# First feed-forward of a two-layer decoder: both experts over all tokens, against tokens sorted by expert with register-addressed weights

## The chip, the cores and the metric

The kernel runs on one core of one Trainium2 chip, as one program with a queue of instructions for each engine: TensorE (PE in the profile), VectorE (DVE), ScalarE (ACT), GpSimd (POOL) and SyncE (SP), which here only issues DMAs. The queues meet only at semaphores. The metric is the device time of one execution in microseconds (us), as the median of several runs.

## The reference

The reference is a decoder of two layers on x of 16 x 64 tokens, 256 wide, in float32. Each layer is a token mixer, a cross-attention and a feed-forward, and each of the six stages is `x = x + stage(layernorm(x))`. The stage that matters here is the feed-forward of the first layer, a mixture of two experts with one picked for each token:

```
logits = x_flat @ w_router.T                       # 1024 tokens x 2
probs = softmax(logits); top_idx = argmax(probs); top_weight = probs[top_idx]
h = einsum('nd,ehd->enh', x_flat, w_fc)            # e = 2 experts, h = 1024, d = 256
a = square(where(h >= 0, h, 0.5 * h))
expert_out = einsum('enh,edh->end', a, w_proj)
mask = (top_idx == expert)
out = einsum('end,en->nd', expert_out, mask * top_weight)
```

It computes both experts for all tokens and keeps one. It is followed by the second layer's self-attention (16 heads of 16 channels, causal, in groups of 64 tokens), whose layernorm needs the feed-forward's result.

## The kernel before

Tokens stand as eight tiles `x[:, t, :]` of 128 rows. They form two halves of 512 (tiles 0 to 3 and 4 to 7) and four pairs g. A layernorm ln is done by pair: `ln_add` adds the stage's result to x and takes the statistics (DVE), `ln_rstd` takes the root (ACT), `ln_scale` writes `xn` (DVE), `ln_turn` transposes it (PE, four transposes for a pair), and `ln_turned` copies it to `xnT` (ACT). ln 2 stands ahead of the first feed-forward, ln 3 ahead of the self-attention.

The order on each queue is written out by hand. Every wait blocks all that stands behind it on the same queue.

Feed-forward before. It is in 32 steps n, sixteen for each half: eight blocks `hb` of 128 hidden units for expert 0, then eight for expert 1, on all 512 tokens of the half. `hidden(n)` (L1222) multiplies the 128 weights' columns by the tokens: 2 matmuls of 512 columns. `leaky(n)` on DVE takes two passes (L1752 and L1755), `hidden_squared(n)` on ACT the square (L682), and `expert_out(n)` (L1238) adds the block to the outputs of its expert in PSUM: 8 recorded instructions, that is 4 matmuls of 256 columns, for the four token tiles. The profile counts two instructions for each float32 matmul. After eight steps `add_expert` (L1762) adds the expert's result, times its weight, to x straight from PSUM. `w_e[e]` is the probability where the token picked expert e, and zero elsewhere. `route` computes the two logits on PE (L1206) and their difference on DVE (L1734 to L1739).

Around it. The cross-attention `cross(0, beside_x0)` runs nine turns `it`, and `beside_x0(it, place)` puts single steps of the norm, of `route` and of the first steps of the feed-forward between its work: `queries` L1074, `keys` L1079, `scores` L1121, `turn_probs` L1132, `context` L1146 and `project_out` L1158 on PE; `shift` L1688 to L1703 and `divide` L1711 to L1715 on DVE; `exps` L614 and `contexts` L655 on ACT. Behind the feed-forward comes the self-attention: `a_project` L1277, `a_values` L1287, then for i from 0 to 7 `a_scores` L1305, `a_shifts` L1831 to L1836 (DVE), `a_exps` L751 (ACT), `a_sums` L1842 (DVE), `a_turn` L1318, `a_turned` L758 (ACT) and `a_context` L1332. i = 0 to 3 belong to the first half, 4 to 7 to the second. POOL adds the bias `a_bo` to x in one instruction (L427) once ln 3 is complete. `weight_sum` (ACT, L771) needs the three weights of the last feed-forward.

All DMAs are issued by SP, most by the helper `load` (L297), in the order of its text. The first stage, a state-space scan, ends at about 280 us; the weight `wvT` of the cross-attention is loaded right behind it.

Of the kernel before, what the change touches and what calls it, by code (L numbers as in the profile page):

```python
# [15 lines left out]
U8 = mybir.dt.uint8  # L16
ALU = mybir.AluOpType
# [23 lines left out]
SHARED = (4, 9, 14)  # L41

# [22 lines left out]
def program(nc, io, out):  # L65
    ctx = ExitStack()
    with ctx:
# [27 lines left out]
        qkb = sb("qkb", [128, 4])  # L95
        ps = ctx.enter_context(nc.psum_tensor("ps", [128, 8, 512], F32))
        region = {"A": sb("region_a", [128, 48 * 256]), "B": sb("region_b", [128, 48 * 256]),
                  "C": sb("region_c", [128, 64 * 256]), "D": sb("region_d", [128, 4 * 256])}
        m_brows = nc.dram_tensor("m_brows", (NK * DST, TOK), F32).ap()
        m_rows = [nc.dram_tensor(f"m_rows{k}", (128, TOK), F32).ap() for k in range(NK)]  # L100
# [72 lines left out]
        f_fc = view("B", 0, [KH, 2 * HID])  # L173
        f_proj = view("B", 16, [2 * HB, D])
        f_neg = [view("C", 32 + 2 * i, [HALF]) for i in range(2)]
        f_leaky = [view("C", 36 + 2 * i, [HALF]) for i in range(2)]
        f_act = [view("C", 40 + 2 * i, [HALF]) for i in range(4)]
# [22 lines left out]
        def ln_bank(ln, g):  # L200

            return tiles2(2 + g % 2 if ln == 3 else g)
# [92 lines left out]
        def _(sp):  # L295
# [15 lines left out]
            load(small[:, 3:5], io["g"], "ld_const")  # L311
            load(qkb[:, :], io["a_bqk"], "ld_const")
            load(m_wout, io["m_wout"], "ld_wout")
# [15 lines left out]
            for u in range(NK * DST):  # L329
# [15 lines left out]
                if k == NK - 1 and n >= 2 and n < DST - 2:  # L345
# [4 lines left out]
                    if n < 6:  # L350
                        load(wk[:, piece], io["x0_wk"][:, piece], "ld_xqk")
                    else:
                        load(wq[:, n // 4 % 2, piece], io["x0_wq"][:, n // 4 % 2, piece], "ld_xqk")
            sp.wait_ge(sem("m_scan"), NK * DST - 1)
# [3 lines left out]
            for name, dst in (("f_router", f_router), ("f_fc", f_fc), ("f_proj", f_proj)):  # L358
                load(dst, io[name], "ld_f")
            sp.wait_ge(sem("ln_xn"), 3 * NT)  # L360
# [6 lines left out]
            for name, dst in (("x1_wvT", wvT1), ("x1_wo", wo1), ("x1_wqT", wqT1), ("x1_wkT", wkT1)):  # L367
                load(dst, io[name], "ld_x1")
            sp.wait_ge(sem("f_h"), 4 * HB)
            for i, name in enumerate(("t_gate", "t_up")):  # L370
                load(t_w[i], io[name], "ld_t")
            sp.wait_ge(sem("f_pr"), 4 * HB)
# [8 lines left out]
        def _(pool):  # L381
# [22 lines left out]
            for u in range(NK * DST - 1):  # L404
# [13 lines left out]
                if k < NK - 1:  # L418
# [4 lines left out]
                    if n == 12:  # L423
                        softplus_sum(k + 1)
            pool.wait_ge(sem("ld_a"), 80)
# [18 lines left out]
        def _(act):  # L444
# [233 lines left out]
            def hidden_squared(n):  # L678
                act.wait_ge(sem("f_leaky"), n + 1)
                if n >= 4:  # L680
                    act.wait_ge(sem("f_pr"), n - 3)
                act.activation(f_act[n % 4], f_leaky[n % 2], ACT.Square).then_inc(sem("f_act"), 1)  # L682
# [1400 lines left out]
```

## Time and profile before

| | |
|---|---|
| median of the runs (lowest, highest) | 960.12 us (959.73, 963.97) |
| the profiled execution's own time | 952.36 us |
| its span | 950.6 us |
| PE busy | 844.8 us (89%) |
| DVE, ACT, POOL busy | 574.7, 436.2, 280.7 us |
| first `hidden` to last `expert_out` | 521.2 to 650.2 us |

The profile is a page of tables and a trace that can be asked for more: a timeline of each engine with the idle time ahead of an instruction and what ended it, the chain of waits that ended last, busy time and granted TensorE clock by stretch, and the DMAs with their time to landing. All times count from the start of the span. Line numbers are those of the kernel before.

### The profile page before, as it was taken

To read this page: it belongs to the slowest core of one execution; us is meant where nothing else is said; L and a number is where in the kernel's file an instruction comes from. 1 tells how busy PE (TensorE), PEld (TensorE's weight loads), DVE (VectorE), ACT (ScalarE), POOL (GpSimd) and SP (SyncE) were. 2 spreads that over 40 slices of the span, in tenths; PEclk is the share of its full clock that TensorE was granted. 3 is DMA by queue.
4 is the path that set the end of the run, shared out by engine and by line. 5 is a ranking of instruction groups with operands and counts; after the bars stand their busy time and mean duration, and the time that the engine had idled before them with its cause. 6 is when DMAs were issued, how large, how long until landed. Compare 5 with 4: busy or idle time off the path is not lost.

```text
span 950.6 us, 12411 instructions
## 1 busy us (share of the span) xinstructions
PE 844.8 (89%) x5114; PEld 515.2 (54%) x5114; DVE 574.7 (60%) x703; ACT 436.2 (46%) x646; POOL 280.7 (30%) x128
## 2 busy tenths in 40 slices
PE   6687797876989899999999999999899899999977
PEld 3233243322445456665666666665788466656755
DVE  3799999899993332223533534545794443474686
ACT  3764655635515655555553221213555322232475
POOL 0189899898850000000000000001006992000000
PEclk9899999998999999999999999999879999999999
DMA  9566666667964000000000070003000000000001
GB/s 312 151 178 177 176 159 188 162 178 188 249 183 177 1 1 1 2 1 1 1 1 2 3 301 1 1 0 133 3 2 2 1 1 1 1 1 1 2 0 45
DMA packets 20120, 70.91 MB, mean 75 GB/s; under 512 B 3072, under 2 KB 4736, under 8 KB 18816
## 3 DMA queue, kind: packets, MB, share of 16 engines
q1 hardware_dynamic: 20064, 70.12, 25.2%
q8 instruction: 40, 0.66, 0.3%
q14 instruction: 16, 0.13, 0.0%
HBM read 66.31 MB, written 3.41 MB: 73 GB/s over the span
## 4 chain that ended last, share of the span: by engine, by line
PE 56%; DVE 15%; ACT 8%; DMA 8%; issue 6%; POOL 6%; SPq 0%; POOLq 0%; DVEq 0%; ACTq 0%
PE ps L1158 10%; PE ps L1074 9%; PE ps L1238 6%; PE ps L1222 6%; DMA region_b<-m_rows 5%; PE ps L1121 3%; POOL region_c L410 3%; PE ps L1146 3%; DMA region_c<-m_rows 3%; PE ps L1079 2%; DVE ps L1641 2%; DVE region_c L1646 2%; PE ps L963 2%; PE ps L1048 2%; PE ps L915 2%
## 5 line engine op out<-in xcount | busy, mean ns | idle before, releaser
L410 POOL TENSOR_TENSOR region_c<-region_c,region_b 128x1024 f32<-128x1024 f32 x42 | 102.8, 2455 | 57.1 <-DMA region_b<-m_rows 46.1
L427 POOL TENSOR_TENSOR x<-x,region_a 128x2048 f32<-128x2048 f32 x1 | 4.5, 4530 | 382.1 <-DVE xn L1555 382.1
L963 PE MATMUL ps<-region_c,ident 128*128 128x512 f32 x168 | 86.8, 644 | 16.8 <-POOL region_c L410 8.5
L1646 DVE TENSOR_TENSOR_SCAN region_c<-region_c,ps 128x1024 f32<-128x1024 f32 x43 | 97.8, 2282 | 2.4 <-ACT ps L559 1.2
L1158 PE MATMUL ps<-region_c 128*128 128x256 f32 x384 | 90.1, 381 | 0.0
L1158 PEld LDWEIGHTS ps<-region_c 128*128 128x128 f32 x384 | 72.4, 190 | 25.0 <-issue 16.8
L1723 DVE COPY region_b<-ps 128x512 f32<-128x512 f32 x32 | 21.5, 689 | 86.9 <-PE ps L1132 86.8
L1641 DVE TENSOR_TENSOR ps<-ps,region_c 128x1024 f32<-128x1024 f32 x52 | 63.2, 1215 | 5.6 <-PE ps L951 5.5
L963 PEld LDWEIGHTS ps<-region_c,ident 128*128 128x128 f32 x168 | 33.1, 204 | 55.3 <-issue 35.4
L1074 PE MATMUL ps<-xnT,region_a 128*128 128x512 f32 x128 | 61.5, 603 | 0.8 <-ACT region_c L627 0.8
L1238 PE MATMUL ps<-region_b,region_c 128*128 128x256 f32 x256 | 60.6, 379 | 0.0
L1222 PE MATMUL ps<-xnT,region_b 128*128 128x512 f32 x128 | 60.2, 593 | 0.0
L1238 PEld LDWEIGHTS ps<-region_b,region_c 128*128 128x128 f32 x256 | 48.6, 190 | 20.1 <-issue 14.9
L1074 PE MATMUL ps<-xnT,region_c 128*128 128x512 f32 x128 | 58.6, 594 | 0.7 <-ACT region_c L655 0.7
L682 ACT ACTIVATE region_c<-region_c 128x512 f32<-128x512 f32 x32 | 20.2, 630 | 84.2 <-DVE region_c L1755 84.2
L1752 DVE TENSOR_SCALAR region_c<-ps 128x512 f32<-128x512 f32 x32 | 22.1, 691 | 55.1 <-PE ps L1222 55.0
L410 POOL TENSOR_TENSOR region_b<-region_c 128x1024 f32<-128x1024 f32 x21 | 51.5, 2453 | 11.8 <-DVE region_c L1646 11.8
L553 ACT ACTIVATE region_c<-region_c,a_log 128x1008 f32<-128x1008 f32 x43 | 47.9, 1127 | 10.0 <-DVE region_c L1646 9.9
L963 PE MATMUL ps<-region_b,ident 128*128 128x512 f32 x84 | 43.6, 643 | 9.7 <-POOL region_b L410 5.4
L951 PE MATMUL ps<-region_b,sel_b 96*128 96x512 bf16 x104 | 32.4, 395 | 21.3 <-DVE region_c L1646 21.2
L1646 DVE TENSOR_TENSOR_SCAN region_c<-region_a,ps 128x1024 f32<-128x1024 f32 x21 | 47.9, 2282 | 2.7 <-issue 1.4
L619 ACT ACTIVATE region_c<-ps 128x512 f32<-128x512 f32 x32 | 19.1, 597 | 64.8 <-PE ps L1074 64.8
(222 smaller groups left out, 1608.5 us busy)
## 6 DMA issues: line engine op xcount, KB each, us to landing
region_b<-m_rows SPq DMA_DIRECT2D x43, 512.0 KB, 5.1
region_c<-m_rows SPq DMA_DIRECT2D x21, 512.0 KB, 5.4
xn<-m_brows SPq DMA_DIRECT2D x12, 512.0 KB, 4.5
region_a<-in_x_wo SPq DMA_DIRECT2D x2, 2048.0 KB, 13.1
m_rows<-region_b SPq DMA_DIRECT2D x4, 512.0 KB, 6.0
region_a<-in_x_wq SPq DMA_DIRECT2D x8, 256.0 KB, 6.8
region_b<-in_f_fc SPq DMA_DIRECT2D x1, 2048.0 KB, 7.9
region_b<-in_f_proj SPq DMA_DIRECT2D x1, 2048.0 KB, 12.9
```

The lines of the kernel that those rows point to most:

```text
L410: pool.tensor_tensor(m_hc[u % 3], m_h[u % 3], m_cb[u % 3], ALU.mult).then_inc(sem("m_hc"), 1)
L553: act.activation(m_da[u % 3][:, :, 1:S], m_delta[k % 2][:, :, 1:S], ACT.Exp, scale=a_log[:, k, n:n + 1]).then_inc(sem("m_da"), 1)
L951: last = pe.matmul(ps[:, 2 * (u % 2) + c, :], sel_b[:, u % 32, :], m_sb[:, u // 32, c * HALF:c * HALF + HALF], start=True, stop=True)
L963: last = pe.matmul(ps[:, 4 + c, :], ident[:, :], m_hc[u % 3][:, c * HALF:c * HALF + HALF], start=(n == 0), stop=(n == DST - 1))
L1074: last = pe.matmul(b, w, xnT[:, k, cols(it)], start=(k == 0), stop=(k == KH - 1))
L1121: last = pe.matmul(ps[64 * (b % 2):64 * (b % 2) + 64, 4 + a // 2, c:c + S], q_T[:, a, S * b:S * b + S], keys_T[:, S * b:S * b + S], start= ...
L1146: last = pe.matmul(banks[r].rearrange("p (s a q) -> p s a q", s=2, a=4)[:, s], ctxn[64 * r:64 * r + 64, 4 * (it // 4) + 2 * m + s, :], mov ...
L1158: last = pe.matmul(tiles2(2 * (it // 4) + t // 2)[:, t % 2, :], o_Ts[layer][it % 2][:, a, 128 * t:128 * t + 128], wvo[:, 4 * (it % 4) + a, ...
L1222: last = pe.matmul(ps[:, 4 + n % 4, :], f_fc[:, k, HID * e + 128 * hb:HID * e + 128 * hb + 128], xnT[:, k, c * HALF:c * HALF + HALF], star ...
L1238: last = pe.matmul(tiles2(2 * e + t // 2)[:, t % 2, :], f_act[n % 4][:, 128 * t:128 * t + 128], f_proj[:, HB * e + hb, :], start=(hb == 0 ...
L1641: dve.tensor_tensor(inputs(u), inputs(u), m_du, ALU.mult).then_inc(sem("m_dbu"), 1)
L1646: dve.tensor_tensor_scan(m_h[u % 3], m_da[u % 3].rearrange("p b t -> p (b t)"), inputs(u), 0.0, ALU.mult, ALU.add).then_inc(sem("m_scan"), 1)
```

## The change

Only the first feed-forward, and what is interleaved with it, is changed. Each half of 512 tokens is now sorted by picked expert. A half takes five tiles of 128 rows, each with tokens of one expert alone (rows that get no token are filled with ones), in whatever way the tokens split. The steps are ten jobs s, five for each half.

- `route(half)` is longer by three operations (the pick, a running count over the four tiles, and what was picked in earlier tiles). `count(half)` on PE counts by three small matmuls with a triangle of ones, and `places(half)` on DVE makes of it, in nine small operations, the row that each token takes (`f_row`) and for each tile the address of its expert's weights (`f_weights_at`).
- POOL scatters the rows of `xn` to DRAM (`scatter`, four indirect DMAs for each half, 128 rows of 1 KB each). SP loads the five tiles back (`sorted_rows`, 640 KB), PE transposes them (`sorted_turn`, ten transposes for each half), ACT copies them (`sorted_turned`).
- `hidden(s)` has the tokens stationary and the weights moving: 4 matmuls of 512 columns. The weights' columns are chosen by a register that PE reads with `value_load`. `leaky(s)` is two passes on DVE of 128x1024. `turn_leaky(s)` is eight transposes on PE, `squared(s)` two squares of 128x512 on ACT, `down_rows(s)` 8 matmuls of 256 columns on PE, `result(s)` a copy of 128x256 on ACT.
- SP stores each result to DRAM, POOL gathers the rows of a half back into `xn` (`gather`, four indirect DMAs), and `add_back(half)` on DVE adds them to x, times the probability. `add_expert` and its weights are gone.
- The DRAM rows are first filled with ones by two DMAs of 640 KB, which SP issues ahead of the load of `wvT`.
- Loads `x1_wo`, `t_gate` and `t_up` wait for the last `hidden`; the other x1 weights are issued behind the store of job 4.
- ln 3 for the first half is done in jobs 7 to 9, for the second half behind `a_scores(2)`, `a_context(0)` and `a_turn(1)`; `a_project(4)` to `a_project(7)` and `a_values(1)` move behind `a_context(1)`.

```diff
+            def count(half):
+                pe.wait_ge(sem("f_pick"), half + 1)
+                b = sort_bank(half)
+                pe.matmul(b[:, 16:20], f_before, small[:, 32 + 4 * half:36 + 4 * half], start=True, stop=False)
+                pe.matmul(b[:, 16:20], ones[:, :], small[:, 84:88], start=False, stop=True)
+                pe.matmul(b[:, 24:25], ones[:, :], small[:, 83:84], start=True, stop=True).then_inc(sem("f_count"), 1)
...
+            def expert_rows(s):
+
+                if s % SORTED == 0:
+                    pe.wait_ge(sem("f_row"), s // SORTED + 1)
+                weights_at.append(pe.value_load(f_weights_at[0:1, s:s + 1], min_val=0, max_val=WEIGHTS))
...
-                for k in range(KH):
-                    last = pe.matmul(ps[:, 4 + n % 4, :], f_fc[:, k, HID * e + 128 * hb:HID * e + 128 * hb + 128],
-                                     xnT[:, k, c * HALF:c * HALF + HALF], start=(k == 0), stop=(k == KH - 1))
+                    pe.wait_ge(sem("f_leaky"), s - 1)
+                expert_rows(s)
+                for c in range(2):
+                    for k in range(KH):
+                        last = pe.matmul(ps[:, 4 + 2 * (s % 2) + c, :], f_xT[h][:, j, k, :],
+                                         f_fc[:, bass.ds(weights_at[s] + (HID * k + HALF * c), HALF)],
+                                         start=(k == 0), stop=(k == KH - 1))
                 last.then_inc(sem("f_h"), 1)
...
-                for t in range(4):
-                    last = pe.matmul(tiles2(2 * e + t // 2)[:, t % 2, :], f_act[n % 4][:, 128 * t:128 * t + 128],
-                                     f_proj[:, HB * e + hb, :], start=(hb == 0 and t % 2 == 0),
-                                     stop=(hb == HB - 1), skip_group_check=True)
+                for hb in range(HB):
+                    last = pe.matmul(ps[:, 2, 0:D], f_aT[s % 2][:, hb, :],
+                                     f_proj[:, bass.ds(weights_at[s] + D * hb, D)],
+                                     start=(hb == 0), stop=(hb == HB - 1))
                 last.then_inc(sem("f_pr"), 1)
...
+            for s in range(2, JOBS - 1):
+                turn_leaky(s)
+                hidden(s + 1)
+                if s == 3:
+                    sorted_turn(1, 0)
+                if s == 4:
+                    sorted_turn(1, 2)
+                if s == JOBS - 2:
                     ln_turn(3, 0)
-                    ln_turn(3, 1)
-                hidden(n)
-                expert_out(n - 2)
...
+                down_rows(s)
+                if s == 3:
+                    sorted_turn(1, 1)
+            pe.wait_ge(sem("ln_T"), 4 * 3 + 1)
+            ln_turn(3, 1)
+            turn_leaky(JOBS - 1)
...
+            def scatter(h):
+                pool.wait_ge(sem("f_fill"), 32)
+                pool.wait_ge(sem("ln_xn"), 2 * NT + 4 * (h + 1))
+                pool.wait_ge(sem("f_row"), h + 1)
+                for t in range(4 * h, 4 * h + 4):
+                    pool.indirect_dma_start(f_in[h], bass.IndirectOffsetOnAxis(ap=f_row[:, t:t + 1], axis=0),
+                                            xn[:, t, :], None).then_inc(sem("f_sent"), 16)
...
             dve.wait_ge(sem("ld_a"), 80)
             a_values(0)
-            ln_scale(3, 2)
-            ln_scale(3, 3)
             a_shifts(0)
             a_shifts(1)
             a_sums(0)
+            add_back(1)
+            ln_add(3, 2)
+            ln_add(3, 3)
+            a_shifts(2)
+            a_sums(1)
+            ln_scale(3, 2)
+            ln_scale(3, 3)
+            a_shifts(3)
+            a_sums(2)
             a_values(1)
```

## Rows read from the trace of the kernel before

**Rows 1.** The page: the span, busy time by engine, granted clock in 40 slices.

```profile
span 950.6 us, 12411 instructions
PE 844.8 (89%) x5114; PEld 515.2 (54%) x5114; DVE 574.7 (60%) x703; ACT 436.2 (46%) x646; POOL 280.7 (30%) x128
PEclk9899999998999999999999999999879999999999
```

**Rows 2.** The chain that ended last, 480 to 760 us: start, us, what.

```profile
582.38 1.73 PE ps L1238 x8
584.11 1.72 PE ps L1222 x4
```

**Rows 3.** Timeline of PE: start, us, instructions, idle before and its releaser.

```profile
292.11 1.88 PE L1074 MATMUL ps<-xnT,region_a 128*128 128x512 f32 x4
493.49 1.84 PE L1206 MATMUL ps<-region_b,xnT 128*128 128x2 f32 x16
514.21 7.17 PE L1158 MATMUL ps<-region_c 128*128 128x256 f32 x32
614.93 1.04 PE L898 MATMUL ps<-ident,xn 128*128 128x128 f32 x8
615.81 1.88 PE L1222 MATMUL ps<-xnT,region_b 128*128 128x512 f32 x4
653.77 3.72 PE L1287 MATMUL ps<-region_b,xnT 128*64 128x256 f32 x32
```

**Rows 4.** The line L1214 (a wait inside `hidden`): when PE's queue passed it.

```profile
L1214 PEldq EVENT_SEMAPHORE  x2: 51/51/51, 517.4 to 523.3; - x2
```

**Rows 5.** Timeline of DVE, 509 to 712 us.

```profile
509.72 0.16 DVE L1735 TENSOR_TENSOR small<-small,ps 128x4 f32<-128x4 f32 x1
641.83 0.69 DVE L1752 TENSOR_SCALAR region_c<-ps 128x512 f32<-128x512 f32 x1 [2.03 <-PE ps L1222]
650.45 1.66 DVE L1762 SCALAR_TENSOR_TENSOR x<-ps,small,x 128x256 f32<-128x256 f32 x4 [7.20 <-PE ps L1238]
658.14 1.37 DVE L1555 TENSOR_SCALAR xn<-x,mv,rstd 128x256 f32<-128x256 f32 x4
659.43 1.22 DVE L1831 TENSOR_TENSOR region_c<-ps,region_a 128x1024 f32<-128x1024 f32 x1
661.93 3.33 DVE L1836 TENSOR_TENSOR region_c<-region_c 128x1024 f32<-128x1024 f32 x1
686.16 1.23 DVE L1831 TENSOR_TENSOR region_c<-ps,region_a 128x1024 f32<-128x1024 f32 x1 [1.17 <-PE ps L1305]
704.30 1.23 DVE L1831 TENSOR_TENSOR region_c<-ps,region_a 128x1024 f32<-128x1024 f32 x1 [0.89 <-PE ps L1305]
```

**Rows 6.** Timeline of ACT, 660 to 680 us.

```profile
671.38 1.06 ACT L751 ACTIVATE region_c<-region_c 128x1024 f32<-128x1024 f32 x1 [1.19 <-DVE region_c L1836]
673.75 1.09 ACT L758 ACTIVATE region_c<-ps 128x512 f32<-128x512 f32 x2 [1.31 <-PE ps L1318]
```

**Rows 7.** Timeline of POOL, 640 to 760 us.

```profile
659.66 4.53 POOL L427 TENSOR_TENSOR x<-x,region_a 128x2048 f32<-128x2048 f32 x1 [382.07 <-DVE xn L1555]
```

**Rows 8.** DMAs: issues with KB each and median us from issue to landing.

```profile
out_x<-x SPq DMA_DIRECT2D x8, 128.0 KB, 1.9
region_b<-in_a_wqkv SPq DMA_DIRECT2D x1, 768.0 KB, 4.3
region_a<-in_x_wvT SPq DMA_DIRECT2D x1, 1024.0 KB, 5.8
```

**Rows 9.** Timeline of SP: start and duration of the issue of `wvT`.

```profile
274.13 0.33 SPq L297 DMA_DIRECT2D region_a<-in_x_wvT  x1
```

**Rows 10.** Stretches of PE: us, busy (instructions), granted clock, DMA share, GB/s.

```profile
678.00:680.00 2.00, 0.60 (x36) 1.00 0.03 8
682.00:684.00 2.00, 2.00 (x32) 0.59 0.03 8
702.00:704.00 2.00, 2.00 (x68) 0.79 0.01 4
```

More of the change, by code:

```diff
@@ L200, in ln_bank @@
         def ln_bank(ln, g):
[L202 removed]
+            if ln == 2 and g >= 2:
+                return tiles2(3 if g == 2 else 1)
+            if ln == 3:
+                return tiles2(2 if g == 2 else 3)
+            return tiles2(g)
         t_w = [view("B", 8 * i, [2048]) for i in range(3)]
@@ L1251, in beside_x0 @@
                     ln_turn(2, 1)
-                if (it, at) == (7, "head 1"):
+                if (it, at) == (7, "begin"):
                     route(0)
+                if (it, at) == (7, "head 2"):
+                    count(0)
+                if (it, at) == (8, "head 2"):
+                    sorted_turn(0, 0)
+                    sorted_turn(0, 1)
                 if (it, at) == (8, "turn"):
@@ L1256, in beside_x0 @@
                 if (it, at) == (8, "context"):
-                    hidden(1)
+                    sorted_turn(0, 2)
                 if (it, at) == (9, "begin"):
-                    expert_out(0)
-                    hidden(2)
-            pe.wait_ge(sem("ld_const"), 64)
+                    turn_leaky(0)
+            pe.wait_ge(sem("ld_const"), 96)
             pe.wait_ge(sem("ld_xqk"), 192)
@@ L1393, in _ @@
                 a_context(i - 2)
+                if i == 3:
+                    pe.wait_ge(sem("ln_T"), 4 * 3 + 4)
+                    for n in range(4, 8):
+                        a_project(n)
+                    a_values(1)
+                    pe.wait_ge(sem("a_qk"), 8)
                 if i <= 8:
                     a_turn(i - 1)
+                if i == 2:
+                    pe.wait_ge(sem("f_y"), JOBS)
+                    ln_turn(3, 2)
+                    ln_turn(3, 3)
                 if i == 6:
@@ L1857, in a_divide @@
                     last.then_inc(sem("a_o"), 1)
-            ln_add(3, 2)
-            ln_add(3, 3)
+            ln_add(2, 2, sem("x0_out"))
+            ln_add(2, 3, sem("x0_out"))
+            ln_scale(2, 2)
+            ln_scale(2, 3)
+            leaky(1)
+            route(1)
+            places(1)
+            route_weights(0)
+            for s in range(2, JOBS):
+                leaky(s)
+                if s == 4:
+                    route_weights(1)
+                if s == 7:
+                    add_back(0)
+                    ln_add(3, 0)
+                    ln_add(3, 1)
+                if s == 8:
+                    ln_scale(3, 0)
+                    ln_scale(3, 1)
             dve.wait_ge(sem("ld_a"), 80)
             a_values(0)
-            ln_scale(3, 2)
-            ln_scale(3, 3)
             a_shifts(0)
```

379 lines of the change are left out of this document (234 added, 145 removed).

## The prediction

> **What bounds the kernel now.** I read the page first, then the chain of waits, then PE's timeline of the stage, and at last the other engines where PE leaves it. The page shows PE busy in 89% of the span, and no other engine over 60% [rows 1]. In the feed-forward the chain is PE alone: steps of 1.72 and 1.73 us alternate with no gap [rows 2], so a pair `hidden`, `expert_out` costs 3.45 us. DVE waits 2.03 us for PE ahead of each of its steps [rows 5]. 32 pairs are 110.4 us. Behind the stage the picture is another one: from `a_scores` on, DVE's passes of 1.22 us, ACT's `a_exps` of 1.06 us and PE take turns [rows 5, 6], and PE is at half its clock (1.2 GHz) from about 682.8 to 702.8 us, after a stretch in which it was busy for 0.60 of 2 us [rows 10]. So two questions decide: how many us of PE work go, and whether the self-attention can start as much earlier as PE does.
>
> **The PE work, part by part.** PE's time goes by the columns of the moving operand: 1024 columns cost 1.72 us, whether as 2 x 512 or as 4 x 256 [rows 2]. A job has 4 x 512 in `hidden` and 8 x 256 in `down_rows`: 3.44 + 3.46 = 6.90 us. Four transposes cost 615.81 - 614.93 = 0.88 us [rows 3], so `turn_leaky` costs 1.76 us. A job is 8.66 us, ten are 86.6 us. The sorted rows cost 20 transposes, 4.4 us. `count` is three matmuls of a few columns; the eight matmuls of `route` take 1.7 us [rows 3], so three take 0.6 us, twice 1.2 us. Sum 92.2 us against 110.4: PE has 18.2 us less to do. `route` only moves.
>
> **Do the other engines keep up within a job?** PE's order is `turn_leaky(s)`, `hidden(s+1)`, `down_rows(s)`. `leaky(s+1)` is two passes of 128x1024 at 1.22 us [rows 5]; with 0.3 us of semaphores some 2.8 us, behind `down_rows` of 3.46 us. Margin 0.6 us. ACT's squares are 2 x 0.55 us [rows 6], with `hidden` of 3.44 us as cover. DVE's extra work in job 7 is `add_back(0)`, 1.66 us (priced as `add_expert`, the same operation), and statistics of two pairs, about 2.2 us; 5.9 us are free between two `leaky`. All of this I put at zero. If `leaky` took 1 us more, 0.4 us a job would show, 4 us in all.
>
> **The way through DRAM at the start.** No row shows an indirect DMA. `places(0)` ends about 502.7 us on the clock of before: `count(0)` lies at 500 us, and nine operations of 0.16 to 0.2 us follow [rows 5]. Then four indirect DMAs, their landing (a store of the same 128 KB lands after 1.9 us), an issue, and a load of 640 KB (768 KB land after 4.3 us) [rows 8]. PE needs the rows behind `project_out(6)` of the third head, about 520.5 us (514.21 plus three quarters of 7 us, plus `count`) [rows 3]. So 17.8 - 1.9 - 0.4 - 4.3 = 11.2 us are left for four issues, 2.8 us each. Bounds from the rows: 0.33 us (a plain issue by SP) [rows 9] and 4.53 us (POOL's longest instruction) [rows 7]. I take 1.5 us, since 128 row addresses are more than SP's issue and far less than a pass over 128x2048: hidden. At 4.53 us each, 7 us would show. In the second half the load stands behind the store of job 2 on SP, which I place about 5 us before PE asks for it: issues and 4.3 us of landing leave 0 to 1.5 us of stall, taken as 0.8. The first steps are ordered anew around `project_out(7)`: `sorted_turn(0, 0)` and `(0, 1)` and two jobs' work fill PE, and waits there come to about 1 us more than before. The fill of 1.3 MB ahead of `wvT` costs nothing: it lands at 274.13 + 5.8 = 279.9 and PE starts the cross-attention at 292.11 [rows 3, 8, 9], so there are 12 us of room; by the 768 KB in 4.3 us the fill takes some 7 us.
>
> So `a_values(0)`, at 653.77 us before [rows 3], comes 18.2 - 0.8 - 1.3 = 16.1 us earlier, at 637.7.
>
> **Registers.** PE must read ten values from SBUF before the matmuls that use them, and compute addresses. What may hide it: PE's queue passed the wait of `hidden(0)` at 517.4 us [rows 4], while the matmuls of `hidden(0)` started at 521.2, so the queue runs 3.8 us ahead where no wait holds it. In a job it is held at `turn_leaky`, for `leaky`, which is free 0.6 us before the array is, and 1.76 us of transposes follow: some 2.4 us, less 0.8 to 1.0 us to issue them, cover about 1.4 us of the read. Bounds: 0.05 us (a wait in that queue) [rows 4], and above by 4.3 us, a whole DMA [rows 8]. I take it as hidden, being nearest to the queue's own rows. The Trainium skill (Runtime: NRT & Kernel Launch, "The ~15µs preamble/postamble breakdown") gives 1.3 us for a register load from HBM, which would be just under this cover; no row here shows one.
>
> **What the tail gives back.** From 637.7 us: `a_values(0)` to 641.4, `a_scores(0)` to 642.6. DVE runs `a_shifts(0)` and `a_shifts(1)` to 650.1 (3 passes of 1.25 us each), `a_sums(0)` to 651.3, `add_back(1)` to 653.0, statistics to 655.0, then, by the written order, `a_shifts(2)` and `a_sums(1)` to 659.9, and only now `ln_scale(3, 2)`, with 0.7 us for its first pair (1.37 us for four tiles [rows 5]). PE is done with `a_turn(1)` at 654.5 and stands at `ln_turn(3, 2)` until 660.6: an idle time of 6 us. The two turns, `a_scores(3)` and `a_context(1)` take it to 664.9, four `a_project` to 671.8, of which one waits about 1.8 us for ACT's copies, `a_values(1)` of 3.7 us and `a_turn(2)` to 678.4, `a_scores(4)` to 679.6. `a_shifts(4)` starts at 679.7; before, it starts at 686.16 [rows 5]. Of 16.1 us, 6.5 are left. What was hidden in PE's surplus before is now DVE's order: `add_expert` was 1.66 us too, but it stood ahead of the attention, with no `a_shifts(2)` between it and `xn`.
>
> The gather isn't late: result 9 is stored by 637.3 (634.7 + 0.4 for the copy, 0.3, 1.9), DVE asks for the rows at 651.3, so each of four indirect DMAs may take 3 us.
>
> Clock. PE stood nearly still about 678.6 to 682 us before, and the half clock followed [rows 10]. The new idle time of 6 us is longer, so I expect the same there, with `ln_turn(3, 2)` to `a_project(5)` at 1.2 GHz: up to 3 us, less the 1.8 us in which PE waits for ACT anyway, about 1.5 us. In return i = 4 to 7 may run at 2.4 GHz. Before, 686.16 to 704.30 us took 18.1 us [rows 5]; DVE alone needs 3 x 4 passes of 1.24 us plus a division of about 2 us, 16.9 us. So -1.2 us to 1.5 us, and I set the two against each other: net 0.
>
> Sum: -6.5 us on a profiled execution of 952.36 us, 945.9 us. The profiled one ran 0.8% under the median of 960.12 us; the same ratio gives 953.6 us.
>
> A rule that speaks against the change, weighed: POOL's bias add from 659.66 to 664.19 stretched a DVE pass that reads two SBUF operands from 1.24 to 3.33 us [rows 5, 7]. The Trainium skill (SBUF — State Buffer, "SBUF: two separate sides") says that the two engines exclude each other for whole instructions, and that descriptors of GpSimd's DMAs can't be written meanwhile. By it, each gather could wait for one pass of `a_shifts` and each scatter for a copy, 4 x 1.24 = 5 us, which the 12 us of room would still take; by the rows alone it is 0.
>
> **Rivals.**
> 1. Register work shows on PE. For it: the cover of 1.4 us is thin and repeated in all jobs. Against it: the queue's lead of 3.8 us. A read of 2.4 us shows 1 us in 9 jobs: +9 us, 962.6 us. From a read of 2.7 us on, the kernel is slower than before by over 0.5%; at 3.2 us 970.
> 2. The way through DRAM is late, the rival on the other side: at over 2.8 us for an indirect DMA PE stands at `sorted_turn(0, 0)`, at over 3 us DVE at `add_back(1)`. At 4.53 us: 7 + 6 = 13 us, 966.6 us, slower. It decides from about 4.2 us.
> 3. The tail gives nothing back, because DVE's passes overlap better than I walked them: up to -16 us, 944 us. Against it: the order on DVE's queue is fixed, so at most part of it.
> 4. The change doesn't make PE's work less as counted: matmuls with an address from a register run slower. 12 in a job, 0.1 us each: +12 us, 965.6 us. Nothing in the trace shows such a matmul.
>
> **How the numbers follow.** Forecast (small gain, 950 to 957 us) 0.55; rival 1 0.18; rival 2 0.10; rival 3 0.10; rival 4 0.07. The range of 948 to 967 us leaves out most of rival 3 and the far ends of 1 and 2. A measurement here tells 0.5% (4.8 us) from no change: faster is below 955.3 us, slower above 964.9 us. Faster: four fifths of the forecast and all of rival 3, 0.54. Slower: half of rivals 1 and 4, most of rival 2, 0.21. The rest, 0.25, is within 0.5%.
>
> **What would show it.** Right: jobs of 8.7 us on PE without gaps; `a_values(0)` near 638 us; an idle time of some 6 us ahead of `ln_turn(3, 2)` put down to DVE's `ln_scale`; the second half's first `a_shifts` near 680 us. Wrong: gaps ahead of each `hidden` with nothing released by another engine (rival 1), PE waiting for a DMA at the first sorted transposes or DVE at `add_back(1)` (rival 2), longer matmuls (rival 4), or an `a_shifts(4)` at 670 us (rival 3).

## The result and the profile after

| | before | after |
|---|---|---|
| median (lowest, highest) | 959.92 us (950.94, 963.97) | 944.95 us (938.76, 948.89) |
| profiled execution, its span | 952.36, 950.6 us | 948.89, 947.0 us |
| PE busy | 844.8 us | 827.5 us |
| `shift(7)` on DVE, the last of the cross-attention, start | 514.37 us | 517.99 us |
| `a_values(0)` on PE, start | 653.77 us | 635.99 us |
| `a_shifts(4)` on DVE, start | 686.16 us | 679.01 us |

The changed kernel takes 0.9863 of the time of before, with an interval of 0.9821 to 0.9904: 1.4% faster, some 13 us. The forecast was 953.6 us with a range of 948 to 967 us, so the direction was right and the gain was larger than the range allowed. Repeats on two chips gave 944.22 us, ratio 0.9879 [0.9851, 0.9907], and 942.09 us, ratio 0.9858 [0.9820, 0.9895]. The gain is 10 to 15 us by medians.

The page of the kernel after, its counterpart to [rows 1]: span, busy time, granted clock in 40 slices, the DMAs with KB and us to landing (POOL's have no KB).

```profile
span 947.0 us, 12500 instructions
PE 827.5 (87%) x5077; PEld 509.5 (54%) x5082; DVE 554.3 (59%) x669; ACT 434.3 (46%) x650; POOL 296.5 (31%) x144
PEclk9899899998999999999999999995889999999989
f_in<-ones SPq DMA_DIRECT2D x2, 640.0 KB, 6.5
region_a<-f_in SPq DMA_DIRECT2D x2, 640.0 KB, 5.2
f_in<-xn,f_row POOLq DMA_INDIRECT x8, 2.4
```

PE is busy for 17.3 us less. The clock's row has 5, 8, 8 where before has 9, 8, 7: PE ran longer at half clock in the self-attention.

PE's timeline of the feed-forward, after (start, us, line, count, idle before and its releaser). L1369 is `turn_leaky`, L1353 `hidden`, L1379 `down_rows`, L1328 `sorted_turn`:

```profile
531.27 1.13 PE L1242 MATMUL ps<-region_b,ctxn 64*128 64x256 f32 x8 [0.82 <-DVE region_b L1883]
533.64 1.13 PE L1242 MATMUL ps<-region_b,ctxn 64*128 64x256 f32 x8 [1.23 <-ACT region_c L721]
553.97 0.38 PE L1311 MATMUL ps<-small,sort 128*128 128x4 f32 x2 [0.51 <-DVE small L1900]
554.93 5.39 PE L1353 MATMUL ps<-region_b,region_a 128*128 x8
560.16 3.62 PE L1379 MATMUL ps<-region_b,region_c 128*128 x16
563.62 1.04 PE L1369 MATMUL ps<-ident,region_c 128*128 128x128 f32 x8
564.49 3.60 PE L1353 MATMUL ps<-region_b,region_a 128*128 x8
571.38 1.04 PE L1369 MATMUL ps<-ident,region_c 128*128 128x128 f32 x8
578.63 0.87 PE L1328 MATMUL ps<-ident,region_a 128*128 128x128 f32 x4 [2.78 <-DMA region_a<-f_in]
579.30 5.13 PE L1379 MATMUL ps<-region_b,region_c 128*128 x16
```

A job is 571.38 - 563.62 = 7.76 us, without a gap. Of it `turn_leaky` is 0.87 us, not the 1.76 us of the forecast. The two `hidden` and `down_rows` at 5.39 and 5.13 us ran partly at 1.2 GHz, each behind a short rest of PE. The wait of 2.78 us is for the load of the second half's sorted rows, which SP issued behind the store of job 2 (L393). The issue alone took 2.17 us:

```profile
571.99 0.32 SPq L393 DMA_DIRECT2D f_out<-region_c  x1
572.41 2.17 SPq L315 DMA_DIRECT2D region_a<-f_in  x1
```

This wait, and where the half clock falls, differ from execution to execution. The first repeat of the changed kernel has:

```profile
575.68 0.66 PE L1328 MATMUL ps<-ident,region_a 128*128 128x128 f32 x4 [1.15 <-DMA region_a<-f_in]
576.17 3.62 PE L1379 MATMUL ps<-region_b,region_c 128*128 x16
```

There the wait is 1.15 us and the `down_rows` behind it runs at full clock. So does `hidden(2)` (3.70 us), behind the same rest of 0.52 us; the half clock fell some 20 us earlier, behind the rests of 0.82 and 1.23 us. The second repeat has a wait of 1.95 us and a `down_rows` of 5.31 us.

The tail, where the self-attention begins (PE, then DVE, after):

```profile
635.99 3.72 PE L1432 MATMUL ps<-region_b,xnT 128*64 128x256 f32 x32
642.19 1.21 PE L1450 MATMUL ps<-region_c 32*64 32x64 f32 x64 [1.33 <-DVE region_c L1983]
645.88 1.94 PE L1463 MATMUL ps<-ident,region_c 128*128 128x128 f32 x8 [2.49 <-ACT region_c L818]
658.54 1.94 PE L994 MATMUL ps<-ident,xn 128*128 128x128 f32 x8 [4.32 <-DVE xn L1715]
664.21 8.93 PE L1422 MATMUL ps<-xnT,region_b 128*128 128x512 f32 x16
657.66 1.37 DVE L1715 TENSOR_SCALAR xn<-x,mv,rstd 128x256 f32<-128x256 f32 x4
679.01 1.23 DVE L1983 TENSOR_TENSOR region_c<-ps,region_a 128x1024 f32<-128x1024 f32 x1 [1.49 <-PE ps L1450]
```

PE stands idle for 4.32 us at `ln_turn(3, 2)` (L994) until DVE's `ln_scale` (L1715), at the place and by the releaser that the forecast named. From `a_values(0)` to `a_shifts(4)` it is 43.0 us; before it was 32.4 us [rows 3, 5], and the forecast had 42.0 us. The two repeats have 44.9 and 43.7 us for it.

The clock there (stretches of PE after: us, busy, granted clock, DMA share, GB/s), to set beside [rows 10]:

```profile
640.00:644.00 4.00, 2.06 (x121) 0.97 1.00 407
644.00:648.00 4.00, 2.12 (x16) 0.50 1.03 421
664.00:668.00 4.00, 4.00 (x17) 0.54 0.02 4
688.00:692.00 4.00, 4.00 (x124) 0.50 0.02 4
```

PE was busy for half of 640 to 644 us. It then ran at 1.2 GHz for 24 us, and again from about 685 to 694 us.

**Where the profiled pair differs.** Split at `shift(7)`, which lies ahead of all the changed PE work but for the first `count`: entry 3.6 us later after; from there to `a_shifts(4)` 171.8 us before and 161.0 us after, so 10.8 us shorter; from `a_shifts(4)` to `a_shifts(7)` 18.1 and 17.8 us; from `a_shifts(7)` to the end 246.3 and 250.2 us. Sum: 3.6 - 10.8 - 0.3 + 3.9 = -3.6 us, the difference of the spans. Of the 3.6 us, 0.6 us are the first `count`. The rest, and the 3.9 us, lie in code that didn't change, and come with short dips of the granted clock that some executions have and others don't. So this pair probably understates the gain. That isn't certain for the 3.9 us: from `a_shifts(7)` to the end both profiled kernels with the old feed-forward take 246.3 us, and the twelve with the new one (without extra scatters) 246.4 to 250.7 us, most of them over 248 us. The stage itself is compared from `shift(7)` on below.

### The profile page after: what moved, and what is told of

Read it like the earlier page. It is cut to its first block, busy times and chain, and to the rows that moved or that the text cites. A ratio compares the mean times of both kernels' runs of the same rounds, so it can differ in the third digit from the quotient of the medians.

```text
span 947.0 us, 12500 instructions
## 1 busy us (share of the span) xinstructions
PE 827.5 (87%) x5077; PEld 509.5 (54%) x5082; DVE 554.3 (59%) x669; ACT 434.3 (46%) x650; POOL 296.5 (31%) x144
## 4 chain that ended last, share of the span: by engine, by line
PE 55%; DVE 16%; DMA 9%; ACT 8%; issue 6%; POOL 6%; SPq 0%; POOLq 0%; DVEq 0%; ACTq 0%
PE ps L1254 11%; PE ps L1170 9%; DMA region_b<-m_rows 5%; PE ps L1217 4%; PE ps L1379 4%; PE ps L1353 3%; PE ps L1242 3%; DMA region_c<-m_rows 3%; POOL region_c L454 3%; PE ps L1175 2%; DVE region_c L1806 2%; DVE ps L1801 2%; POOL region_b L454 2%; PE ps L1059 2%; PE ps L1422 2%
## 5 line engine op out<-in xcount | busy, mean ns | idle before, releaser
L475 POOL DMA_INDIRECT f_in<-xn,f_row x8 | 8.0, 994 | 276.3 <-DVE f_row L1917 274.5
L685 ACT ACTIVATE region_c<-ps 128x512 f32<-128x512 f32 x32 | 19.1, 597 | 66.6 <-PE ps L1170 66.6
L1011 PE MATMUL ps<-xnT,region_b 128*128 128x512 f32 (+1 forms) x96 | 45.9, 611 | 0.7 <-ACT xnT L526 0.7
L688 ACT ACTIVATE region_c<-ps 128x512 f32<-128x512 f32 x32 | 19.1, 597 | 58.4 <-PE ps L1170 58.4
L1848 DVE TENSOR_TENSOR region_c<-ps,small 128x1024 f32<-128x1024 f32 x8 | 9.8, 1225 | 54.4 <-PE ps L1217 54.4
L721 ACT ACTIVATE region_c<-ps 128x512 f32<-128x512 f32 x48 | 25.4, 598 | 34.8 <-PE ps L1242 34.8
L501 POOL TENSOR_SCALAR region_b<-region_b,small 128x512 f32<-128x512 f32 x12 | 25.1, 2088 | 49.2 <-PE ps L1488 49.2
## 6 DMA issues: line engine op xcount, KB each, us to landing
region_a<-in_x_wo SPq DMA_DIRECT2D x2, 2048.0 KB, 10.8
```

Source lines behind the costliest of these rows:

```text
L1011: last = pe.matmul(ps[0:rows, pair_at + c, :], lhs(k), (rhs if rhs is not None else xnT[:, k, :])[:, c * HALF:c * HALF + HALF], start=(k = ...
```

## The experiments

In what follows "from `shift(7)`" is the time from the start of that pass (`divide` and the feed-forward follow it) to the start of the `a_shifts` named, in the profiled execution. It is 145.1 us to `a_shifts(0)` and 171.8 us to `a_shifts(4)` before; 122.9 and 161.0 us after. In the first repeat of the changed kernel it is 120.1 and 159.0 us, and that repeat is what the variants are compared with. The second repeat has 122.6 and 160.5 us, so a difference of 2 us between two profiles can be chance. "The tail" is the stretch from `a_values(0)` to `a_shifts(4)`: 32.4 us before, 43.0, 44.9 and 43.7 us in the three profiles of the changed kernel.

> The changed kernel again, as the base for the others on the same chip. Theory T: the job is 7.76 us, since eight transposes cost 0.88 us and not 1.76, and a half clock falls where PE stands idle. Expected: 12 to 14 us below the kernel before. Rival R (the gain of the first runs was luck of the clock): 6 to 8 us below.

Measured: 944.22 us, ratio 0.9879 [0.9851, 0.9907], 10.3 us below by medians. That is less than theory T expected and more than the rival did.

**1. The transposes, doubled.**

```diff
-                    for a in range(4):
+                    for a in (0, 1, 2, 3) * 2:
```

> Each of the eight transposes of turn_leaky is written twice; the output is unchanged. T (0.11 us a transpose, PE is the limit through all jobs): a job of 8.64 us, a_values(0) about 8.8 us later, the time 7 to 9 us above the changed kernel. Rival (0.22 us a transpose, as the prediction had it): 17 us more. Rival (the tail is set by DVE and swallows it): under 3 us more.

Measured: 946.74 us, ratio 0.9921 [0.9896, 0.9947], 2.5 us more by medians. PE's timeline:

```profile
559.42 1.91 PE L1369 MATMUL ps<-ident,region_c 128*128 128x128 f32 x16
568.05 1.91 PE L1369 MATMUL ps<-ident,region_c 128*128 128x128 f32 x16
573.90 0.66 PE L1328 MATMUL ps<-ident,region_a 128*128 128x128 f32 x4 [0.50 <-DMA region_a<-f_in]
```

Sixteen transposes take 561.16 - 559.42 = 1.74 us, 0.109 us each, and a job 568.05 - 559.42 = 8.63 us. That is the job of the forecast (8.66 us), with twice the transposes that the kernel has. So the size of the error is shown. The time moved less than the 8.7 us of work: 5.5 us to `a_shifts(0)`, 5.2 us to `a_shifts(4)`, 2.5 us by medians. Part of it went into rests that were there anyway: the wait for the sorted rows is 0.50 us where the repeat has 1.15 us, and the rest of 0.52 us ahead of `count(1)` is gone. Another part is chance: the repeat ran two short rows ahead of `project_out(7)` at half clock, 1.6 us longer, and this run didn't. The expected 7 to 9 us of time were wrong.

**2. The load of the second half's rows, one store earlier.**

```diff
-            for s in range(3):
+            for s in range(2):
...
-            for s in range(3, SORTED):
+            for s in range(2, SORTED):
```

> SP issues the load of the second half's sorted rows ahead of the store of job 2 instead of behind it. T: PE's wait of 2.8 us at sorted_turn(1, 0) is gone, and with it the half clock of the 5 us behind it, 3 to 4.5 us lower. Rival (the load is late for the scatter's sake): the wait stays, within 1 us.

Measured: 942.86 us, ratio 0.9872 [0.9849, 0.9895]. The wait is gone:

```profile
573.46 0.60 PE L1328 MATMUL ps<-ident,region_a 128*128 128x128 f32 x4
573.89 3.62 PE L1379 MATMUL ps<-region_b,region_c 128*128 x16
```

From `shift(7)` it is 118.7 us to `a_shifts(0)` and 156.7 us to `a_shifts(4)`, 1.4 and 2.3 us less than in the repeat. By medians it is 1.4 us less, which the intervals don't separate from nothing. The expected 3 to 4.5 us counted on the wait and the slow `down_rows` of the first profile, and the repeat has only the 1.15 us of wait.

**3. Addresses written out in place of the register.** The three first jobs of a half take expert 0 and the last two expert 1, whatever the tokens picked.

```diff
-                weights_at.append(pe.value_load(f_weights_at[0:1, s:s + 1], min_val=0, max_val=WEIGHTS))
+                weights_at.append(WEIGHTS * (s % SORTED >= 3))
```

> The changed kernel with constants in place of the register: value_load is left out, the first three tiles of each half take expert 0's weights and the last two expert 1's, so the result is right for tokens whose tile happens to have that expert only; all other work is the same. T (PE's queue runs ahead, a register operation is 46 ns): jobs of 7.76 us as before, the time within 1 us of the changed kernel. Rival 1 of the prediction (register work shows): jobs shorter by 0.5 us or more, 5 us lower.

Measured: 941.06 us, ratio 0.9860 [0.9824, 0.9895]; the kernel with registers has 0.9879 and 0.9858. A job takes 7.76 us here too (`turn_leaky` starts at 562.76 and 570.52 us), so inside the jobs the registers cost nothing. From `shift(7)` it is 119.2 us to `a_shifts(0)` against 120.1 us. The rows of the kernel after for the lines of the read and of `hidden`: duration in ns (min, median, max), first and last start.

```profile
L1338 PEldq TENSOR_LOAD <-f_weights_at x10: 298/302/490, 524.6 to 615.4; - x10
L1353 PEldq FUSED_REGOPS  x40: 42/46/51, 525.5 to 616.4; - x40
L1353 PE MATMUL ps<-region_b,region_a x80: 592/592/1145, 525.8 to 619.8; 128*128 x80
```

A read is 0.30 us and an address 0.046 us, both in PE's queue, under a cover that the forecast put at 1.4 us. The matmul itself takes 0.592 us (median), and with a fixed address 0.592 us too.

**4. The old kernel with less PE work and its own tail.** One of eight blocks of hidden units is left out for each expert, so 4 of 32 pairs, 13.8 us by the 3.45 us of a pair.

```diff
+FB = HB - 1
...
-                c, e, hb = n // (2 * HB), n // HB % 2, n % HB
+                c, e, hb = n // (2 * FB), n // FB % 2, n % FB
```

> The kernel before with seven of the eight hidden blocks of each expert (one eighth of the first feed-forward's hidden units is left out): 28 steps for 32, 13.8 us less on PE, with the old order of the tail. Theory T (the new order of the tail takes back what PE gains): with the old order nearly all passes to the end, 12 to 14 us below the kernel before. Rival (the self-attention is set by DVE whatever stands ahead of it): 6 us or less.

Measured: 938.81 us, ratio 0.9835 [0.9800, 0.9870], 14.9 us less than before by medians. From `shift(7)` it is 131.3 us to `a_shifts(0)` and 157.9 us to `a_shifts(4)`, 13.8 and 13.9 us less than before. The tail is 32.3 us, as before. So the old tail hands on all that PE saves. The new one doesn't: PE reaches `a_values(0)` 21.4 us earlier (118.0 against 139.4 us from `shift(7)`), and 10.8 us are left at `a_shifts(4)`. That a tail gives nothing back is possible; this one gives back half.

**5. `ln_scale(3, 2)` and `(3, 3)` ahead of `a_shifts(2)`.**

```diff
-            a_shifts(2)
-            a_sums(1)
             ln_scale(3, 2)
             ln_scale(3, 3)
+            a_shifts(2)
+            a_sums(1)
```

> On DVE's queue ln_scale(3, 2) and (3, 3) stand ahead of a_shifts(2) and a_sums(1). T (the tail gives the gain back in DVE's order): ln_turn(3, 2) starts 3.5 to 4.5 us earlier, a_shifts(4) too, the time 3 to 4 us lower. Rival (the work of a_shifts(2) is only moved and delays a_scores(3) as much): within 1 us.

Measured: 944.35 us, ratio 0.9867 [0.9835, 0.9898], and `a_shifts(4)` comes 156.5 us after `shift(7)` against 159.0 us, of which 1.0 us lies ahead of the tail. By medians the expected gain of 3 to 4 us didn't come (944.35 against 944.22 us). PE's timeline:

```profile
649.54 1.92 PE L994 MATMUL ps<-ident,xn 128*128 128x128 f32 x8
651.38 1.37 PE L1450 MATMUL ps<-region_c 32*64 32x64 f32 x64
657.74 1.91 PE L1477 MATMUL ps<-region_c 64*64 64x16 f32 x64 [4.98 <-ACT region_c L825]
```

The idle time ahead of `ln_turn` (L994) is gone, and one of 4.98 us stands ahead of `a_context(1)`. ACT's `a_turned(1)` (L825) is written behind `a_exps(2)`, which now waits for the later `a_shifts(2)`. One queue was reordered, and the next one became the wait.

**6. The tail reordered on all three engines.** Experiments 2 and 5 together, with ACT's `a_turned(1)` and both `ln_turned` ahead of `a_exps(2)`, and two of the four `a_project` ahead of `a_scores(3)`:

```diff
-            a_exps(2)
...
+            a_exps(2)
+            projected(4)
+            projected(5)
...
+                if i == 3:
+                    pe.wait_ge(sem("ln_T"), 4 * 3 + 4)
+                    a_project(4)
+                    a_project(5)
```

> The load of e3 first, ln_scale(3, 2) and (3, 3) ahead of a_shifts(2) as in e2, and with it ACT's a_turned(1) and ln_turned(3, 2), (3, 3) ahead of a_exps(2), and PE's a_project(4), (5) ahead of a_scores(3). T: in e2 PE's idle time only moved to a_context(1), behind ACT's a_exps(2); with ACT and PE in order too, PE works through it: a_shifts(4) 4 to 6 us earlier than in e3, the time 3 to 5 us below e3. Rival (DVE's passes set the tail): within 1.5 us of e3.

> The kernel with the reordered tail again, as the base for the next one on the same chip: 15 to 18 us below the kernel before.

Measured: 936.99 us, ratio 0.9817 [0.9776, 0.9858], and on another chip 937.91 us, ratio 0.9821 [0.9795, 0.9847]. From `shift(7)` it is 149.7 and 151.8 us to `a_shifts(4)` against 156.7 us in experiment 2. The tail alone takes 38.2 and 39.1 us against 44.0 us. PE no longer waits for `xn`:

```profile
645.97 1.91 PE L996 MATMUL ps<-ident,xn 128*128 128x128 f32 x8
648.57 5.89 PE L1424 MATMUL ps<-xnT,region_b 128*128 128x512 f32 x8 [0.69 <-ACT xnT L526]
656.58 3.70 PE L1424 MATMUL ps<-xnT,region_b 128*128 128x512 f32 x8
```

So 5 to 6 of the 11 us that the tail gave back were due to the order of its steps. The row of 5.89 us is two `a_project`, partly at 1.2 GHz; the same two take 3.70 us at 2.4 GHz.

**7. The old order of the tail, behind the new feed-forward** (`ln_scale` and all of `a_project` and `a_values` ahead of the attention steps, with experiment 2's load).

> The changed kernel with the load of e3 first and with the order of the kernel before in the tail: on DVE add_back(1) and ln 3 of the second half ahead of a_shifts(0), on PE ln_turn(3, 2) and the last projections behind a_scores(0), on ACT likewise. T (the way through DRAM at the end is the price, and the new order was a way round it): DVE stands at add_back(1) until the gather has landed, near 641 us for 635, so some 6 us of PE and DVE idle, but a_shifts(4) still within 3 us of e3's. The time within 4 us of e3. Rival (the new order alone takes the gain back): a_shifts(4) 6 us or more earlier than in e3, near 667 us, the time at least 5 us below e3.

Measured: 941.06 us, ratio 0.9865 [0.9825, 0.9906]. The DVE row and the PE row that it leads to:

```profile
640.03 1.67 DVE L1934 SCALAR_TENSOR_TENSOR x<-xn,small,x 128x256 f32<-128x256 f32 x4 [5.88 <-DMA xn<-f_out,f_row]
644.47 1.94 PE L991 MATMUL ps<-ident,xn 128*128 128x128 f32 x8 [8.90 <-DVE xn L1711]
```

Here the gather isn't covered: DVE waits 5.88 us for it and PE stands still for 8.90 us. To `a_shifts(4)` it is 159.3 us from `shift(7)`, 2.6 us more than with the new order (156.7 us), but by times the two can't be told apart. The new order hides the gather and pays for it elsewhere, about as much.

**8. PE kept busy in its rests,** by matmuls of 256 columns into an unused bank. In the first kernel only this is added (2, 4 and 8 of them), in the second it stands on experiment 6 (2, 5 and 3).

```diff
+            def keep_busy(count):
+                for _ in range(count):
+                    pe.matmul(ps[:, 3, 0:256], ident[:, :], xnT[:, 0, 0:256], start=True, stop=True)
```

> The changed kernel with 14 matmuls of 256 columns that nobody reads, put where PE stands idle in the tail: 2 ahead of a_scores(1), 4 ahead of a_turn(0), 8 ahead of ln_turn(3, 2); 6 us of work at 2.4 GHz into idle times of 8 us. C (the half clock of about 30 us behind the feed-forward costs time): the clock stays at 2.4 GHz from 636 to 668 us, a_project(4) to (7) take 6.9 us for 8.9 us, the time 3 to 5 us lower. Rival (PE isn't the limit there): within 1 us, or up to 2 us slower where the extra matmuls stand in the way.

> The reordered tail, and ten matmuls that nobody reads in PE's idle times behind a_values(0). C: the clock stays at 2.4 GHz to about 670 us, a_project(4) and (5) take 3.4 us for 5.9 us, a_shifts(4) 2 to 4 us earlier, the time 1 to 4 us lower. Rival (the later idle times bring the half clock anyway, and DVE is the limit): within 1 us.

Measured: 940.30 us, ratio 0.9853 [0.9811, 0.9895], and 935.36 us, ratio 0.9812 [0.9783, 0.9842]. The clock answers. In the first kernel the half clock comes later and is short, and it returns further on (clock, then PE's rows):

```profile
640.00:644.00 4.00, 2.92 (x76) 1.00 1.02 421
644.00:648.00 4.00, 2.22 (x67) 0.76 0.15 59
680.00:684.00 4.00, 4.00 (x80) 0.50 0.02 4
653.81 1.30 PE L994 MATMUL ps<-ident,xn 128*128 128x128 f32 x8 [0.86 <-DVE xn L1722]
657.24 3.70 PE L1422 MATMUL ps<-xnT,region_b 128*128 128x512 f32 x8
662.66 3.70 PE L1422 MATMUL ps<-xnT,region_b 128*128 128x512 f32 x8 [1.73 <-ACT region_c L810]
```

`a_shifts(4)` comes 157.8 us after `shift(7)` against 159.0 us, and the tail takes 40.9 us against 43.0 to 44.9 us, with some 20 us more at full clock. From `ln_turn(3, 2)` to the first of the four `a_project` PE takes 3.43 us (653.81 to 657.24), and 5.67 us in the first profile of the changed kernel (658.54 to 664.21). The four `a_project` gain nothing: at full clock PE waits 1.73 us for ACT's copies in their middle, and they take 9.06 us against 8.86 us without that wait, partly at half clock. In the second kernel the clock is full until about 668 us, and the tail takes 37.1 us against 38.2 and 39.1 us. By times neither kernel differs from the one without the matmuls. So with the clock kept up the tail is 2 to 4 us shorter in one kernel and 1 to 2 us in the other. The added matmuls stand in PE's queue too, so what the clock costs alone stays unmeasured.

**9. The scatter, doubled.** Each half's four scatters are also sent to a second buffer, ahead of the useful ones, and SP's load waits for all eight.

```diff
+                    pool.indirect_dma_start(f_dup[h], bass.IndirectOffsetOnAxis(ap=f_row[:, t:t + 1], axis=0),
+                                            xn[:, t, :], None).then_inc(sem("f_sent"), 16)
```

> Each scatter is issued twice, once into a DRAM tensor that nobody reads, and all must have landed before the sorted rows are loaded: 5 us more on POOL in each half. T (the way in is hidden: the rows of the first half have landed some 5 us before PE turns them, and in the second half SP's store order decides, not the scatter): within 1.5 us of the changed kernel. Rival 2 of the prediction (the way through DRAM decides): 4 to 10 us slower.

> The doubled scatters again, for one look at ScalarE: in the first look it stood idle for 3.0 us near 516 us with nothing of this core ahead of it, while the second half of the scatters was under way. If the scatters cause it, an idle time of 2 to 4 us stands there again; if it was chance, none does.

Measured: 948.62 us, ratio 0.9930 [0.9903, 0.9957], some 4 to 7 us slower than the changed kernel (its repeats were on other chips); a single run on another chip gave 947.8 us. The first sorted rows weren't late for PE. What is new stands on ACT, and ahead of PE:

```profile
519.12 2.06 ACT L724 ACTIVATE region_c<-ps 128x512 f32<-128x512 f32 x4 [3.04 <-remote]
520.46 2.09 PE L1220 MATMUL ps<-region_c 128*64 128x64 f32 x64 [3.35 <-ACT region_c L724]
```

The same two rows in the first repeat of the changed kernel:

```profile
513.76 2.06 ACT L721 ACTIVATE region_c<-ps 128x512 f32<-128x512 f32 x4 [0.62 <-PE ps L1242]
515.10 2.08 PE L1217 MATMUL ps<-region_c 128*64 128x64 f32 x64 [0.52 <-ACT region_c L721]
```

The single run has the row with 2.32 us, as it was expected to if the scatters are the cause.

**10. The extra scatters behind the useful ones,** counted by a semaphore for which no load waits (only the gathers at the end of a half), so that the load goes out as early as in the changed kernel.

> The changed kernel again, as the base for the doubled scatters on the same chip: 10 to 13 us below the kernel before.

> Each half's four useful scatters first, then the four that nobody reads, for which only the gathers wait: as much traffic and POOL work as with doubled scatters, but the sorted rows are loaded as early as in the changed kernel. Theory L (latency of the way in costs): the time within 1 us of the changed kernel. Theory C (scatters under way disturb other queues, whatever waits for them): 3 to 5 us slower, with an idle time of ScalarE or another engine near 516 us.

Measured: the changed kernel 942.09 us, ratio 0.9858 [0.9820, 0.9895], 15.1 us below by medians and so more than expected; with the later scatters 950.24 us, ratio 0.9928 [0.9897, 0.9959], 8.2 us above it. The row is there again:

```profile
515.93 2.06 ACT L726 ACTIVATE region_c<-ps 128x512 f32<-128x512 f32 x4 [2.33 <-remote]
```

It isn't ACT alone. In the same run DVE stands still in the second half, where the changed kernel has 5.22 us for PE at this pass, and PE waits behind it:

```profile
571.82 1.23 DVE L1935 TENSOR_SCALAR region_c<-ps 128x1024 f32<-128x1024 f32 x1 [7.72 <-remote]
574.36 1.10 PE L1374 MATMUL ps<-ident,region_c 128*128 128x128 f32 x8 [1.62 <-DVE region_c L1938]
```

So it isn't the later load. The profile has no releaser on this core for these waits ("remote"). They stand in all three profiles with extra scatters and in none of the fourteen without. At the first place ACT goes on 1.29 to 1.34 us behind the end of the row of POOL's last scatter in all three. The runs don't tell what ACT and DVE wait for.

In the profile of experiment 10 the rows add up to about 6 us on PE against the repeat on the same chip: 3.1 us at the first place, 1.6 us more for the rows right behind it, at half clock, 1.6 us at the second place. Yet this profiled execution took 945.23 us, as long as the repeat's (945.33 us): it was one of the fastest of twelve, with fewer dips of the clock elsewhere. So a loss of 4 to 8 us by medians is of the size of these rows, but no profile shows where the slower executions lose it. Whether the scatters that the changed kernel needs cost it something in the same way is open too. No idle time of this kind shows in its profiles.

## Why the forecast was off

**PE's work: the step that failed.** The price of a transpose was read from the row of L898 at 614.93 us [rows 3]. Its "x8" was taken for the recorded instructions of one `ln_turn`, with two for each transpose as for each float32 matmul. But a transpose is recorded once, and the row held both `ln_turn(3, 0)` and `ln_turn(3, 1)`: eight transposes in 0.88 us, not four. So `turn_leaky` was 0.87 us and not 1.76, and a job 7.76 us and not 8.66. Ten jobs and twenty sorted transposes come to 77.6 + 2.2 us, with the 1.2 us of `count` 81.0 us. The work removed is 110.4 - 81.0 = 29.4 us where the forecast had 18.2 us. Experiment 1 gives 0.109 us for a transpose and rebuilds the forecast's job to 0.03 us by doubling them. The check was at hand: the code there issues two turns, and the line's count over the whole kernel (80 for twenty turns) gives four instructions for each turn of four transposes.

**The start and the stall: too small.** The first `count` lies ahead of `shift(7)`, so 30.0 us less work lie behind it. At `a_values(0)` the profile has 21.4 us from `shift(7)`, so 8.6 us are lost on the way, where the forecast subtracted 2.1 us (0.8 us and 1.3 us, though its text has about 1 us for the latter). Rows show 7.2 of the 8.6 us: the wait for the second half's rows, 2.78 us against 0.8 (PE went on 6.2 us after the load's issue began, where 4.3 us were taken for the landing), the rests around `project_out(7)` and `count(1)` (0.82, 1.23 and 0.51 us, where before has 0.21 and 1.26 us), and the half clock, 1.8 and 1.5 us over the 3.6 us of the same work. The last wasn't in the forecast at all. The repeats lose 4.7 and 7.3 us in all. A part of the stall follows from the first error: `turn_leaky(3)` stands between the store of job 2 and `sorted_turn(1, 0)`, and it covers 0.9 us less than was thought. Experiment 1, with a wait of 0.50 us, agrees.

**Do the other engines keep up: right.** Jobs run without a gap, as the rows of 563.62 to 575.7 us show.

**The way through DRAM at the start: right.** A scatter takes POOL 0.96 us and 0.30 us between two, 1.26 us each against 1.5 taken; the scatters land after 2.4 us (1.9 taken), the load is issued at 512.65 us and PE needs its rows at 523.16 us. The fill landed after 6.5 us (7 estimated) and held nobody up. Rival 2 as it was put, data that come late for `sorted_turn(0, 0)` or `add_back(1)`, didn't occur. But indirect DMAs do have a price that the forecast had only in waiting for data: experiments 9 and 10 show 4 to 8 us for eight more, with ACT and DVE standing still. The Trainium skill (SBUF — State Buffer, "SBUF: two separate sides") would have let scatters wait for DVE; POOL's rows show 0.96 us with 0.30 us between them, so nothing of that size, and what the doubled scatters held up was ACT and DVE, not POOL. No run here isolates that rule for descriptors.

**Registers: right.** Rival 1 is refuted by experiment 3: the job is 7.76 us with and without them. The read is 0.30 us (TENSOR_LOAD). The Trainium skill (Runtime: NRT & Kernel Launch, "The ~15µs preamble/postamble breakdown") had 1.3 us for a load from HBM; this one is from SBUF and shorter, and the measurement decides. Rival 4 is refuted by the same run: 0.592 us for a matmul in both.

**The tail: right in place and size.** 42.0 us were walked and 43.0 us measured, 9.6 us of give-back forecast (16.1 - 6.5) and 10.6 measured (43.0 - 32.4). The walk had one idle time of 6 us; the profile has 4.32 us there and 1.33 and 2.49 us ahead of it. Experiment 5 shows that DVE's order alone doesn't explain it, since ACT's order takes over. Experiment 6 gets 5 to 6 us of it back by changing all three. Rival 3 was wrong for this tail, though its figure of 944 us is close to the measured 944.95 us: the gain came from PE's work, and the tail did give half of it back. Experiment 4 shows a tail that gives nothing back, the old one.

**The clock: wrong in extent, some 2 us too small.** The forecast had about 8 us at 1.2 GHz and a gain later; the profile has 24 us and another 9 us, and `a_shifts(4)` to `a_shifts(7)` gained only 0.3 us. It was right that PE waits about 1.8 us for ACT's copies in `a_project`, so that the half clock is free there: experiment 8 has 1.73 us. Ahead of it, from `ln_turn(3, 2)` on, the half clock cost 2.2 us that the forecast didn't count. That the tail still came out within 1 us is in part luck: the rest of the walk was about 1 us too long.

**The sum, redone.** 30.0 us less PE work behind `shift(7)`, 8.6 us lost ahead of `a_values(0)`, 10.6 us in the tail: -10.8 us in the profile at `a_shifts(4)`, and -12.8 and -11.3 us in the repeats, against -6.5 us forecast. Medians have 10 to 15 us. The error of 11.2 us in PE's work was partly made good by errors the other way, in the start, the stall and the tail; with those right and the transposes as they were, the forecast would have been further off. The forecast's own time was also tied to a before of 960.12 us, of three runs; later series of 11 to 17 runs had medians of 953.7 to 957.2 us, so the profiled execution of 952.36 us was less of an exception than its 0.8% made it look.

## What to carry to other kernels

Before a duration is divided by a count, find out from the code how many calls the row holds and how many instructions the profile records for one operation; a transpose and a float32 matmul differ by two here. Where an engine is relieved, walk the next stage in written order on every queue: here half of the gain was lost there, moving one engine's steps only moved the wait, and moving three engines' steps got 5 to 6 us back. And before two profiles are compared, find out how far two profiles of one kernel differ: here by 2 us at `a_shifts(4)`, and by 1.6 us in a single wait. The version of experiment 6, best with the matmuls of experiment 8, takes 935.4 to 937.9 us, 1.8 to 1.9% below the kernel before and some 0.5% below the changed one, with intervals that overlap in part.

## What the runs showed of the hardware

- A transpose of 128x128 in float32 takes PE 0.109 us in a stream and is one recorded instruction.
- PE reads a register from SBUF in 0.30 us and computes an address in 0.046 us, in its queue, and matmuls with such an address keep their 0.592 us.
- An indirect DMA of 128 rows of 1 KB takes POOL 1.26 us with the pause behind it, and lands after 2.4 us (scatter) or 6.7 us (gather beside large loads).
- Eight more scatters made the kernel 4 to 8 us slower, also where only the gathers wait for them; ACT stood still for 2.3 to 3.0 us at one place, and in one run DVE 2.5 us longer than its 5.2 us at another. The mechanism is open.
- 1.2 GHz came behind waits of PE of 2.78 and 1.95 us (`down_rows` 5.13 and 5.31 us in place of 3.6) and not behind 1.15 and 0.50 us. Behind the same rest of 0.5 us `hidden(2)` took 5.39 us in one profile and 3.70 us in both repeats, so a rest's length alone doesn't decide it.
